# Recommender kernel on one core: gathered rows laid out by field, and both DRAM copies of a block in one transfer

## The chip, the cores and the metric

The kernel runs on one core of one Trainium2 chip. The metric is device time in microseconds (us) of one execution; smaller is better. Before the change three runs took 361.72, 362.16 and 364.56 us, median 362.16. One per cent of that is 3.6 us.

## The reference

512 samples have 32 fields each. Every field has its own table of rows of 16 numbers, and one row per sample and field is gathered. Then follow three interaction layers and a small multilayer perceptron, all in float32:

```python
e = jnp.stack([tbl_0[ids[:, 0]], tbl_1[ids[:, 1]], ...], axis=1)   # (512, 32, 16)
for W in (W0, W1, W2):                                             # W0 (32,32,64), W1 and W2 (32,64,64)
    xk = jax.nn.relu(jnp.einsum('bmd,bhd,mhk->bkd', x0, xk, W))
    outs.append(jnp.sum(xk, axis=2))                               # (512, 64) per layer
h = jnp.concatenate([z, dense_ctx], axis=1)                        # z is outs side by side, 192 wide
h = jnp.maximum(h @ W_top1 + b_top1, 0.0)                          # 512 wide
h = jnp.maximum(h @ W_top2 + b_top2, 0.0)                          # 256 wide
y = h @ W_top3
```

## The kernel before, in words

**Blocks.** The batch is cut into eight pairs of 32-sample chunks. Pairs 0 and 1 are worked in two halves each (blocks 0 to 3, 512 columns of sample times dimension, called half-width or narrow); pairs 2 to 7 are one block each (blocks 4 to 9, 1024 columns, wide). Each block goes through layers 0, 1 and 2; a step is written (layer, block), and the tuple `BEGUN` (L53) is the order of the 30 steps on VectorE and TensorE. Even pairs use one set of SBUF buffers, odd pairs the other ("streams").

**A step.** VectorE (DVE, `product`, L760) multiplies tiles of x0 with a factor that lies in PSUM and writes `vz`; GpSimd (POOL, L705) makes some of these products into `pz`; TensorE (PE, `contract`, L993) multiplies them with the weights and sums up in `acc`; ScalarE (ACT, L876) takes the relu, and L887 sends the result round to all partitions as `hidden`. Some factors are spread by TensorE instead (L924), for blocks 1 to 3 in layer 0 at L938, and for block 0 straight from the gathered rows (L960, L963). DVE sums over the 16 dimensions at L810. The numbers of tiles that each engine takes, and the gathers between them, are tables (`POOL_TILES`, `GATHERS_IN`, `PACED`, `BEHIND_SPREAD`) that the change leaves alone.

**Gathering.** POOL adds to every id the first row of its field's table (`index`, L709, one operation on all 128 columns) and issues 128 indirect transfers (L678). One brings a row of 16 floats to each of the 128 partitions: 32 fields times four quarters of a block's samples. A wide block has 16 of them, a narrow one 8. Partition `q * 32 + m` holds field m of quarter q.

**The DRAM scratch.** The operands of the products need each field's whole row on four or more partitions. So SyncE's queue (SP) writes every block's gathered rows to DRAM as 32 rows by field, twice (`scratch`, L558; the second copy stands behind the first, so that a read rotated by r fields does not wrap), and reads them back with access patterns that repeat or rotate fields:

```python
for c in range(1 if b in DIRECT else 2):
    copy = fields_dram[b][c * FIELDS:(c + 1) * FIELDS, :]
    sp.dma_start(copy.rearrange("m (q x) -> q m x", q=QUART), quarter_rows(b)) ...
```

`layer0_operands` issues `own` (L574, needs the first copy), `opposite` (L582, needs the second), and for wide blocks four `rotated` tiles (L593); `field_tiles` issues eight `fields_sb` tiles (L614). Rotated and field tiles are sent with at most three in flight: the fourth waits until the first has landed. All of this stands in one queue in the order of `LOADS` (L105): a wait in it holds back all that stands behind, and that order has `scratch 4, operands 4, fields 3, scratch 5, operands 5, fields 4`.

**Opposite fields.** Layer 0 uses symmetry; the pair of fields m and m + 16 is made by POOL (`opposite_product`, L688, into `oz`) from the gathered rows and `opposite`, and contracted with `w0c_sb` (L989), whose rows follow the partition layout of the gathered rows.

Of the kernel before, what the change touches and what calls it, by code (L numbers as in the profile page):

```python
# [11 lines left out]
P = 128  # L12
# [19 lines left out]
BLOCKS = [(pair, half * N, N, half * GATHERS // 2, GATHERS // 2) for pair in range(2) for half in range(2)]  # L32
BLOCKS += [(pair, 0, PAIR, 0, GATHERS) for pair in range(2, PAIRS)]
# [4 lines left out]
def stream(b):  # L38
    return BLOCKS[b][0] % STREAMS

# [339 lines left out]
def cin_dlrm(nc, table, ids, first_row, unit, turned, across, w0a, w0b, w0c, w1, w2, wt1, bt1, wt2,  # L380
             bt2, wt3, wt1_dense, dense, out):
    with ExitStack() as ctx:
# [6 lines left out]
        def sem(name):  # L389
            return ctx.enter_context(nc.semaphore(name))  # L390
# [6 lines left out]
        first_sb = sb("first_sb", [P, 1], I32)  # L397
# [15 lines left out]
        w0c_sb = sb("w0c_sb", [P, QUART, HID])  # L413
# [28 lines left out]
        scratch_in = [[sem(f"scratch_in{b}_{c}") for c in range(1 if b in DIRECT else 2)] for b in range(len(BLOCKS))]  # L442
# [64 lines left out]

        def landed(b):

            return 16 * (turn(b) + 1)  # L510
# [26 lines left out]
        def _(sp):  # L537
# [7 lines left out]
            sp.dma_start(w0c_sb[:, :, :], w0c).then_inc(w0_in, 16)  # L545
# [6 lines left out]
            def scratch(b):  # L552

                pair, _, _, first, rows = BLOCKS[b]
                sp.wait_ge(rows_in[b], 16 * rows)
                for c in range(1 if b in DIRECT else 2):
                    copy = fields_dram[b][c * FIELDS:(c + 1) * FIELDS, :]
                    sp.dma_start(copy.rearrange("m (q x) -> q m x", q=QUART),  # L558
                                 quarter_rows(b)) \
                      .then_inc(scratch_in[b][c], 16)  # L560

            def layer0_operands(b):
                _, col, cols, _, _ = BLOCKS[b]
                span, s = fields_dram[b], stream(b)
                sp.wait_ge(scratch_in[b][0], 16)
# [6 lines left out]
                if second_half(b):  # L572
# [23 lines left out]
            def field_tiles(b):  # L596
# [6 lines left out]
                sp.wait_ge(scratch_in[b][0], 16)  # L603
# [42 lines left out]
        def _(pool):  # L646
# [6 lines left out]
            def gather(i):  # L653
# [3 lines left out]
                if j == 0 and pair >= GRING:  # L657
                    before = max(a for a in range(len(BLOCKS)) if BLOCKS[a][0] == pair - GRING)
                    for a in range(before):
                        if BLOCKS[a][0] == pair - GRING:  # L660
                            pool.wait_ge(vz_ready, vectors_to((0, a)))
                            pool.wait_ge(scratch_in[a][0], 16)
                            if a not in DIRECT:
                                pool.wait_ge(pz_ready, pools_to((0, a)))
                                pool.wait_ge(scratch_in[a][1], 16)
                    pool.wait_ge(scratch_in[before][0], 16)
                    if before in DIRECT + BURST:
                        pool.wait_ge(vz_ready, vectors_to((0, before)))
                    if before not in DIRECT:
                        pool.wait_ge(scratch_in[before][1], 16)  # L670
                        pool.wait_ge(pz_ready, pools_to((0, before)))
# [4 lines left out]
                if i in BEHIND_SPREAD:  # L676
                    pool.wait_ge(factor_spread, BEHIND_SPREAD[i])
                nc.gpsimd.indirect_dma_start(  # L678
# [13 lines left out]
            def product(step, u):  # L692
# [10 lines left out]
                if at >= PRING:  # L703
# [210 lines left out]
        def _(pe):  # L914
# [52 lines left out]
            def contract(step, who, u, start, stop):  # L967
# [17 lines left out]
                if layer == 0 and t == L0TILES:  # L985
                    pieces = []
                    for q in (0, 2, 1, 3):
                        part = slice(q % 2 * quarter, (q % 2 + 1) * quarter)
                        last = nc.tensor.matmul(acc_of(step, q // 2)[:, part], w0c_sb[:, q, :], quarters,  # L989
# [167 lines left out]
```

## Time and profile before

| what | us |
|---|---|
| median of three runs | 362.16 |
| span of the profiled execution, first to last instruction | 340.6 |
| median less span (start and end of the program; the page gives no other time of the profiled execution) | 21.6 |
| TensorE busy | 304.3 (89%) |
| VectorE busy | 281.9 (83%) |
| GpSimd busy | 245.8 (72%) |
| ScalarE busy | 49.1 (14%) |
| SP's queue waiting for the DRAM copies before `own` (L574) | 26.6 |
| DVE at L760 waiting for `fields_sb` / for `rotated` | 5.2 / 1.8 |

Busy time is the sum of an engine's instructions. Idle time of an engine is put down to what released it. All instants below are counted from the span's start.

### The profile page before, as it was taken

How to read it: one execution, taken by the hardware profiler on the slowest of the kernel's cores; microseconds unless marked ns; L12 is line 12 of the kernel's file. 1: busy time of each engine (PE TensorE's matmuls, PEld its weight loads, DVE VectorE, ACT ScalarE, POOL GpSimd, SP SyncE). 2: the span in 40 equal slices, each digit the busy share in tenths (PEclk: the TensorE clock that was granted, in tenths of full speed). 3: DMA queues.
4: the chain of work that ended last, by engine and by line, in shares of the span. 5: the costliest groups of instructions: out<-in, count | busy, mean ns of one | idle time of the engine just before them, and what ended most of it. 6: DMA issues, size and time to landing. Idle time of an engine off the chain costs nothing.

```text
span 340.6 us, 4674 instructions
## 1 busy us (share of the span) xinstructions
PE 304.3 (89%) x1798; PEld 126.1 (37%) x1798; DVE 281.9 (83%) x172; ACT 49.1 (14%) x70; POOL 245.8 (72%) x194
## 2 busy tenths in 40 slices
PE   0198888989968898989999999999999999999997
PEld 0164554644423253233333333233333333333334
DVE  0038899999969799999999999989998879999210
ACT  1010002110111110110211301220131012020011
POOL 4656777877756878899979598979977678649200
PEclk9997999999989999999999999999999999999999
DMA  6264865738768888685899994943898996230000
GB/s 188 47 194 100 248 184 178 223 71 244 230 185 258 309 283 291 225 253 173 285 346 308 330 320 138 287 130 108 259 365 305 310 289 175 39 102 0 2 0 0
DMA packets 34040, 67.96 MB, mean 200 GB/s; under 512 B 5602, under 2 KB 14946, under 8 KB 34018
## 3 DMA queue, kind: packets, MB, share of 16 engines
q1 hardware_dynamic: 23298, 56.64, 49.9%
q10 hardware_dynamic: 6624, 9.96, 10.3%
q0 software_dynamic: 4096, 1.06, 3.7%
q8 instruction: 14, 0.23, 0.3%
q14 instruction: 8, 0.07, 0.1%
HBM read 55.38 MB, written 2.03 MB: 169 GB/s over the span
## 4 chain that ended last, share of the span: by engine, by line
PE 44%; DMA 25%; DVE 17%; issue 7%; POOL 2%; SPq 2%; ACTq 1%; ACT 1%; DVEq 1%
PE acc L993 34%; DVE vz L760 16%; DMA fields_sb<-fields 12%; DMA rotated<-fields 5%; DMA fields<-gathered 3%; DMA hidden<-relu_out 3%; POOL gathered L678 2%; PE factor L1005 2%; PE factor L924 2%; DMA gathered<-in_table,index 2%; PE factor L960 1%; PE factor L1000 1%; PE acc L989 1%; PE factor L938 1%; DVE feats L810 1%
## 5 line engine op out<-in xcount | busy, mean ns | idle before, releaser
L760 DVE TENSOR_TENSOR vz<-fields_sb,factor 128x1024 f32<-128x1024 f32 (+3 forms) x113 | 230.7, 2092 | 15.4 <-PE factor L924 8.0
L993 PE MATMUL acc<-vz,w_sb 128*64 128x512 f32 (+1 forms) x1232 | 227.5, 509 | 16.6 <-DVE vz L760 15.7
L678 POOL DMA_INDIRECT gathered<-in_table,index x128 | 121.6, 950 | 45.1 <-issue 27.8
L993 PEld LDWEIGHTS acc<-vz,w_sb 128*64 128x64 f32 x1232 | 87.5, 140 | 142.3 <-issue 90.0
L705 POOL TENSOR_TENSOR pz<-fields_sb,hidden 128x1024 f32<-128x1024 f32 (+1 forms) x52 | 118.0, 2291 | 23.3 <-DMA hidden<-relu_out 9.0
L993 PE MATMUL acc<-pz,w_sb 128*64 128x512 f32 (+1 forms) x208 | 50.7, 579 | 0.7 <-POOL pz L705 0.7
L876 ACT ACTIVATE relu_out<-acc 128x512 f32<-128x512 f32 (+1 forms) x30 | 15.3, 511 | 152.4 <-PE acc L993 123.7
L845 ACT ACTIVATE factor<-hidden 128x1024 f32<-128x1024 f32 (+1 forms) x23 | 20.1, 879 | 69.5 <-DVE vz L760 34.1
L760 DVE TENSOR_TENSOR vz<-rotated,factor 128x2048 f32<-128x2048 f32 x12 | 27.0, 2282 | 3.0 <-DMA rotated<-fields 1.8
L993 PEld LDWEIGHTS acc<-pz,w_sb 128*64 128x64 f32 x208 | 14.8, 137 | 29.9 <-issue 24.2
L810 DVE TENSOR_REDUCE feats<-relu_out 128x32 f32<-128x512 f32 (+1 forms) x30 | 17.2, 573 | 6.6 <-ACT relu_out L876 6.5
L960 PE MATMUL factor<-gathered,unit_sb 32*128 32x128 f32 x8 | 1.6, 493 | 15.4 <-DMA gathered<-in_table,index 15.4
L924 PE MATMUL factor<-relu_out,unit_sb 32*128 32x512 f32 (+1 forms) x68 | 11.0, 539 | 0.5 <-ACT relu_out L876 0.5
L777 DVE TENSOR_TENSOR vz<-own,factor 128x512 f32<-128x512 f32 x2 | 1.4, 689 | 11.2 <-ACT own L851 11.2
L989 PE MATMUL acc<-oz,w0c_sb 128*64 128x256 f32 (+1 forms) x72 | 8.2, 348 | 0.5 <-POOL oz L688 0.5
L845 ACT ACTIVATE factor<-own 128x1024 f32<-128x1024 f32 x6 | 6.2, 1026 | 13.4 <-POOL pz L705 8.5
L859 ACT ACTIVATE hidden<-factor 128x1024 f32<-128x1024 f32 (+1 forms) x4 | 3.7, 919 | 24.4 <-PE factor L924 24.4
L824 DVE TENSOR_SCALAR vz<-factor,bt_sb 128x512 f32<-128x512 f32 x2 | 1.5, 751 | 6.7 <-PE factor L1012 6.7
L960 PEld LDWEIGHTS factor<-gathered,unit_sb 32*128 32x128 f32 x8 | 1.0, 306 | 15.4 <-issue 15.4
L989 PEld LDWEIGHTS acc<-oz,w0c_sb 128*64 128x64 f32 x72 | 4.7, 137 | 5.4 <-issue 2.9
L924 PEld LDWEIGHTS factor<-relu_out,unit_sb 32*128 32x128 f32 x68 | 3.7, 183 | 7.7 <-issue 6.8
L729 DVE TENSOR_TENSOR w_sb<-vz 128x256 f32<-128x256 f32 x1 | 0.4, 425 | 7.0 <-DMA w0c_sb<-in_w0c 7.0
(36 smaller groups left out, 61.9 us busy)
## 6 DMA issues: line engine op xcount, KB each, us to landing
fields_sb<-fields SPq DMA_DIRECT2D x48, 512.0 KB, 5.7
rotated<-fields SPq DMA_DIRECT2D x24, 512.0 KB, 6.0
fields_sb<-fields SPq DMA_DIRECT2D x32, 256.0 KB, 3.5
hidden<-relu_out ACTq DMA_DIRECT2D x30, 256.0 KB, 5.4
own<-fields SPq DMA_DIRECT2D x6, 512.0 KB
gathered<-in_table,index POOLq DMA_INDIRECT x128, 4.1
hidden<-relu_out ACTq DMA_DIRECT2D x16, 128.0 KB, 4.3
fields<-gathered SPq DMA_DIRECT2D x12, 128.0 KB
```

Of the source, the lines that this page charges most:

```text
L678: nc.gpsimd.indirect_dma_start(gathered[:, pair % GRING, j, :], None, table, bass.IndirectOffsetOnAxis(ap=index[:, i:i + 1], axis=0)).then ...
L705: nc.gpsimd.tensor_tensor(pz[:, at % PRING, 0:cols], fields[s][:, t, col:col + cols], hidden_of(step, g), ALU.mult).then_inc(pz_ready, 1)
L760: nc.vector.tensor_tensor(vz[:, at:at + nt, 0:cols].rearrange("p t (a n) -> p t a n", n=half), src[:, t:t + nt, col:col + cols].rearrange( ...
L810: nc.vector.tensor_reduce(feats[layer][:, pair, first:first + count], relu_of(step).rearrange("p (b d) -> p b d", d=DIM), op=ALU.add, axis ...
L845: nc.scalar.activation(factor_of(step, g), src.rearrange("p (a n) -> p a n", a=2), ACT.Copy).then_inc(factor_put, 1)
L859: nc.scalar.activation(hidden_of(step, g).rearrange("p (a n) -> p a n", a=2), factor_of(step, g), ACT.Copy).then_inc(hidden_copied, 1)
L876: nc.scalar.activation(relu_of(step), acc[:, n % 2, 0:half], ACT.Relu).then_inc(relu_done, 1)
L924: last = nc.tensor.matmul(factor_of(step, g)[:, ab, :], unit_sb[row:row + HROWS, :], relu_of(before)[row:row + HROWS, :], start=True, stop ...
L960: last = nc.tensor.matmul(slot_of(step, held)[:, ab, wave * quarter:(wave + 1) * quarter], by, rows[row, :], start=True, stop=True)
L989: last = nc.tensor.matmul(acc_of(step, q // 2)[:, part], w0c_sb[:, q, :], quarters, start=False, stop=q % 2 == 1)
L993: last = nc.tensor.matmul(acc_of(step, ab), w_sb[layer][:, kt, :], z[:, ab * half:(ab + 1) * half], start=start and j == 0, stop=stop and ...
L1005: return nc.tensor.matmul(to, wt2_sb[:, k, m * P:(m + 1) * P], rows, start=k == 0, stop=k == F_TOP1 // P - 1)
```

## The change

Wide blocks (`by_field(b)` is 1) now have field m, quarter q on partition `4 * m + q`. The ids are sorted that way on the host, `first_row` has a second column for this layout, and `w0c_sb` holds a second version. For these blocks partition p's part lies at DRAM offset p * 256 elements, so one transfer with 128 partitions as its outer dimension writes both copies (256 runs of 1 KB), and `opposite` is read with the same outer 128. Narrow blocks keep their layout; their copies are written in four transfers of 32 partitions, each for both copies (one copy for block 0). There is one semaphore per block, so `own` now waits for both copies. The index addition is split: 32 columns first, the other 96 after the first 21 gathers.

```diff
-                for c in range(1 if b in DIRECT else 2):
-                    copy = fields_dram[b][c * FIELDS:(c + 1) * FIELDS, :]
-                    sp.dma_start(copy.rearrange("m (q x) -> q m x", q=QUART),
-                                 quarter_rows(b)) \
-                      .then_inc(scratch_in[b][c], 16)
+                cols, span, n = BLOCKS[b][2], fields_dram[b], scratch_copies(b)
+                if by_field(b):
+                    twice = bass.AP(span.tensor, span.offset,
+                                    [[cols // QUART, P], [FIELDS * cols, n], [1, cols // QUART]])
+                    sp.dma_start(twice, quarter_rows(b)[:, None, :].broadcast_to([P, n, cols // QUART])) \
+                      .then_inc(scratch_in[b], 16)
+                    return
+                for q in range(QUART):
+                    twice = bass.AP(span.tensor, span.offset + q * (cols // QUART),
+                                    [[cols, FIELDS], [FIELDS * cols, n], [1, cols // QUART]])
+                    mine = quarter_rows(b)[q * FIELDS:(q + 1) * FIELDS, None, :]
+                    sp.dma_start(twice, mine.broadcast_to([FIELDS, n, cols // QUART])).then_inc(scratch_in[b], 16)
...
-                sp.wait_ge(scratch_in[b][0], 16)
+                sp.wait_ge(scratch_in[b], copied(b))
...
-                sp.wait_ge(scratch_in[b][1], 16)
                 far = bass.AP(span.tensor, span.offset + FIELDS // 2 * cols,
-                              [[quarter, QUART], [cols, FIELDS], [1, quarter]])
+                              [[quarter, P], [1, quarter]] if by_field(b)
+                              else [[quarter, QUART], [cols, FIELDS], [1, quarter]])
...
-            nc.gpsimd.tensor_tensor(index[:, :], ids_sb[:, :], first_sb[:, :].broadcast_to([P, PAIRS * GATHERS]),
-                                    ALU.add).then_inc(index_ready, 1)
+            narrow = NARROW_PAIRS * GATHERS
+            nc.gpsimd.tensor_tensor(index[:, 0:narrow], ids_sb[:, 0:narrow],
+                                    first_sb[:, 0:1].broadcast_to([P, narrow]), ALU.add).then_inc(index_ready, 1)
             pool.wait_ge(index_ready, 1)
             for i in range(FIRST_GATHERS):
                 gather(i)
+            nc.gpsimd.tensor_tensor(index[:, narrow:], ids_sb[:, narrow:],
+                                    first_sb[:, 1:2].broadcast_to([P, PAIRS * GATHERS - narrow]),
+                                    ALU.add).then_inc(index_ready, 1)
...
+        def copied(b):
+            return 16 if by_field(b) else 16 * QUART
```

How instructions move. SP's queue, from the first copy of block 0 to block 1's reads, before (L558 is the copy; `4x32x128` is its DRAM side):

```order
L558 DMA fields<-gathered 4x32x128 [waits rows_in0]
L614 DMA fields_sb<-fields 128x1x512 [waits scratch_in0_0]
...
L558 DMA fields<-gathered 4x32x128 [waits rows_in1]
L558 DMA fields<-gathered 4x32x128
L574 DMA own<-fields 128x1x512 [waits scratch_in1_0]
L582 DMA opposite<-fields 128x1x128 [waits scratch_in1_1]
```

and the same place with the change (L580 is the copy of a narrow block, L594 `own`, L602 `opposite`):

```order
L580 DMA fields<-gathered 32x128 [waits rows_in0]
L580 DMA fields<-gathered 32x128 x3
L634 DMA fields_sb<-fields 128x1x512 [waits scratch_in0]
...
L580 DMA fields<-gathered 32x2x128 [waits rows_in1]
L580 DMA fields<-gathered 32x2x128 x3
L594 DMA own<-fields 128x1x512 [waits scratch_in1]
L602 DMA opposite<-fields 128x1x128
```

Block 0 issues four copies instead of one, blocks 1 to 3 four instead of two, and `opposite` has no wait of its own any more. At the first wide block (block 4) SP's queue has with the change (L573 is the copy, L613 `rotated`):

```order
L573 DMA fields<-gathered 128x2x256
L594 DMA own<-fields 128x1x1024
L602 DMA opposite<-fields 128x256
L613 DMA rotated<-fields 128x1x1024 x4
L634 DMA fields_sb<-fields 128x1x512 x8
```

where two copies of form `4x32x256` stood. GpSimd, from the index addition to block 1's opposite product, with the change:

```order
L730 TENSOR_TENSOR index<-ids_sb,first_sb 128x32
L698 DMA gathered<-in_table,index 128x16 x21
L735 TENSOR_TENSOR index<-ids_sb,first_sb 128x96
L698 DMA gathered<-in_table,index 128x16 x2
L708 TENSOR_TENSOR oz<-gathered,opposite 128x128
L698 DMA gathered<-in_table,index 128x16 x11
```

Before, one addition of form 128x128 stood ahead of 23 gathers. TensorE, VectorE and ScalarE keep their instructions and their order.

## Rows read from the trace of the kernel before

**Rows 1.** Busy time by stretch: us, PE, PEld, DVE, ACT, POOL, PE clock, DMA share, GB/s

```profile
90.00:105.00 15.00, 11.42 (x80) 5.46 (x80) 11.46 (x11) 1.30 (x2) 9.70 (x11) 0.89 0.65 189
105.00:120.00 15.00, 12.28 (x78) 4.81 (x76) 13.15 (x10) 2.39 (x4) 12.07 (x14) 1.00 0.85 292
120.00:140.00 20.00, 19.07 (x128) 8.55 (x124) 20.00 (x12) 3.04 (x4) 15.15 (x14) 1.00 0.87 296
180.00:200.00 20.00, 20.00 (x98) 6.82 (x96) 20.00 (x10) 4.20 (x5) 16.56 (x9) 1.00 0.97 312
260.00:280.00 20.00, 19.15 (x98) 6.36 (x96) 16.04 (x8) 2.22 (x3) 14.14 (x7) 1.00 0.91 304
```

**Rows 2.** VectorE in order of time: start, us, instruction, [idle before, releaser]

```profile
50.40 2.35 DVE L800 TENSOR_TENSOR vz<-own,factor 128x1024 f32<-128x1024 f32 x2 [0.63 <-DMA own<-fields]
...
95.21 1.22 DVE L760 TENSOR_TENSOR vz<-fields_sb,factor 128x1024 f32<-128x1024 f32 x1 [1.18 <-DMA fields_sb<-fields]
98.09 1.22 DVE L760 TENSOR_TENSOR vz<-fields_sb,factor 128x1024 f32<-128x1024 f32 x1 [1.66 <-DMA fields_sb<-fields]
99.59 2.88 DVE L760 TENSOR_TENSOR vz<-fields_sb,factor 128x1024 f32<-128x1024 f32 x2 [0.28 <-DMA fields_sb<-fields]
...
114.87 2.29 DVE L760 TENSOR_TENSOR vz<-rotated,factor 128x2048 f32<-128x2048 f32 x1 [1.84 <-DMA rotated<-fields]
```

**Rows 3.** SP's queue in order of time: start, us of issuing, transfer, count

```profile
15.30 0.69 SPq L558 DMA_DIRECT2D fields<-gathered  x1
17.84 7.86 SPq L614 DMA_DIRECT2D fields_sb<-fields  x8
29.33 1.17 SPq L558 DMA_DIRECT2D fields<-gathered  x2
32.00 0.56 SPq L574 DMA_DIRECT2D own<-fields  x1
32.81 0.54 SPq L582 DMA_DIRECT2D opposite<-fields  x1
...
42.06 1.17 SPq L558 DMA_DIRECT2D fields<-gathered  x2
47.56 0.56 SPq L574 DMA_DIRECT2D own<-fields  x1
...
72.67 1.17 SPq L558 DMA_DIRECT2D fields<-gathered  x2
76.16 0.56 SPq L574 DMA_DIRECT2D own<-fields  x1
77.51 0.54 SPq L582 DMA_DIRECT2D opposite<-fields  x1
78.10 7.35 SPq L593 DMA_DIRECT2D rotated<-fields  x4
85.54 10.98 SPq L614 DMA_DIRECT2D fields_sb<-fields  x8
96.57 1.17 SPq L558 DMA_DIRECT2D fields<-gathered  x2
```

**Rows 4.** Chain of waits between 76 and 116 us: start, us, what

```profile
78.10 6.82 DMA rotated<-fields
...
108.35 6.40 DMA rotated<-fields
```

**Rows 5.** Busy time by stretch, columns as in rows 1: two copies' transfers

```profile
72.70:76.00 3.30, 3.01 (x26) 1.66 (x26) 3.30 (x5) 0.38 (x1) 2.48 (x3) 1.00 0.22 52
206.30:209.60 3.30, 3.30 (x18) 1.11 (x16) 3.30 (x2) 0.00 (x0) 2.67 (x4) 1.00 0.25 53
```

**Rows 6.** GpSimd in order of time

```profile
3.35 0.40 POOL L709 TENSOR_TENSOR index<-ids_sb,first_sb 128x128 int32<-128x128 int32 x1 [2.90 <-DMA first_sb<-in_first_row]
...
37.00 0.47 POOL L688 TENSOR_TENSOR oz<-gathered,opposite 128x128 f32<-128x128 f32 x1
...
93.28 0.74 POOL L688 TENSOR_TENSOR oz<-gathered,opposite 128x256 f32<-128x256 f32 x1
```

More of the change, by code:

```diff
@@ L28 @@
 TOP_LOADS = 9 * 16
-BLOCKS = [(pair, half * N, N, half * GATHERS // 2, GATHERS // 2) for pair in range(2) for half in range(2)]
-BLOCKS += [(pair, 0, PAIR, 0, GATHERS) for pair in range(2, PAIRS)]
+NARROW_PAIRS = 2
+BLOCKS = [(pair, half * N, N, half * GATHERS // 2, GATHERS // 2) for pair in range(NARROW_PAIRS) for half in range(2)]
+BLOCKS += [(pair, 0, PAIR, 0, GATHERS) for pair in range(NARROW_PAIRS, PAIRS)]
 LAST = len(BLOCKS) - 1
@@ L39, in stream, with by_field, scratch_copies @@
     return BLOCKS[b][0] % STREAMS
+def by_field(b):
+    return int(BLOCKS[b][0] >= NARROW_PAIRS)
+def scratch_copies(b):
+    return 1 if b in DIRECT else 2
 def blocks_before(b):
@@ L412, in cin_dlrm @@
         across_sb = sb("across_sb", [P, P])
-        w0c_sb = sb("w0c_sb", [P, QUART, HID])
+        w0c_sb = sb("w0c_sb", [P, 2, QUART, HID])
         w_sb = [sb("w0_sb", [P, L0TILES, HID]),
@@ L441, in cin_dlrm @@
         rows_in = [sem(f"rows_in{b}") for b in range(len(BLOCKS))]
-        scratch_in = [[sem(f"scratch_in{b}_{c}") for c in range(1 if b in DIRECT else 2)] for b in range(len(BLOCKS))]
+        scratch_in = [sem(f"scratch_in{b}") for b in range(len(BLOCKS))]
         own_in = [sem(f"own_in{s}") for s in range(STREAMS)]
@@ L544, in _ @@
             sp.dma_start(w0b_sb, w0b).then_inc(w0_in, 16)
-            sp.dma_start(w0c_sb[:, :, :], w0c).then_inc(w0_in, 16)
+            sp.dma_start(w0c_sb[:, :, :, :], w0c).then_inc(w0_in, 16)
             sp.dma_start(w_sb[1][:, :, :], w1).then_inc(w1_in, 16)
@@ L661, in gather @@
                             pool.wait_ge(vz_ready, vectors_to((0, a)))
-                            pool.wait_ge(scratch_in[a][0], 16)
+                            pool.wait_ge(scratch_in[a], copied(a))
                             if a not in DIRECT:
                                 pool.wait_ge(pz_ready, pools_to((0, a)))
-                                pool.wait_ge(scratch_in[a][1], 16)
-                    pool.wait_ge(scratch_in[before][0], 16)
+                    pool.wait_ge(scratch_in[before], copied(before))
                     if before in DIRECT + BURST:
@@ L677, in gather @@
                     pool.wait_ge(factor_spread, BEHIND_SPREAD[i])
+                if i == NARROW_PAIRS * GATHERS:
+                    pool.wait_ge(index_ready, 2)
                 nc.gpsimd.indirect_dma_start(
@@ L988, in contract @@
                         part = slice(q % 2 * quarter, (q % 2 + 1) * quarter)
-                        last = nc.tensor.matmul(acc_of(step, q // 2)[:, part], w0c_sb[:, q, :], quarters,
+                        last = nc.tensor.matmul(acc_of(step, q // 2)[:, part], w0c_sb[:, by_field(b), q, :], quarters,
                                                 start=False, stop=q % 2 == 1)
@@ L1095 @@
                      .reshape(ids[pair].shape))
-    ids = np.ascontiguousarray(ids.transpose(1, 3, 0, 2).reshape(P, PAIRS * GATHERS))
-    first_row = np.ascontiguousarray(np.tile(first.astype(np.int32), QUART)[:, None])
+    ids = np.concatenate([ids[:NARROW_PAIRS].transpose(1, 3, 0, 2).reshape(P, NARROW_PAIRS * GATHERS),
+                          ids[NARROW_PAIRS:].transpose(3, 1, 0, 2).reshape(P, (PAIRS - NARROW_PAIRS) * GATHERS)],
+                         axis=1)
+    first_row = np.stack([np.tile(first.astype(np.int32), QUART), np.repeat(first.astype(np.int32), QUART)], axis=1)
     w0 = np.asarray(inputs["L0_rec_W0"])
```

12 lines of the change are left out of this document (6 added, 6 removed).

## The prediction, made before the changed kernel ran

> **What bounds the kernel now.** I read the busy time by stretch first, because an average over the whole span (TensorE 89%, VectorE 83%) hides that the bound moves. From 120 us on some engine is always full: VectorE has 20.00 of 20 us in 120 to 140, both engines have 20.00 in 180 to 200, and in 260 to 280 VectorE is down to 16.04 while TensorE has 19.15 [rows 1]. Moving transfers there can give back at most TensorE's missing 0.85. Between 90 and 120 neither is full: VectorE 11.46 and 13.15 of 15, TensorE 11.42 and 12.28, and TensorE's granted clock falls to 0.89 in 90 to 105 [rows 1]. So I asked VectorE's order of time what it waits for there: three waits for field tiles of block 3 (1.18 + 1.66 + 0.28 = 3.12 us) and one for a rotated tile of block 5 (1.84 us); earlier there is one of 0.63 for block 2's `own` [rows 2]. These 5.59 us are what faster transfers can win; everything behind them is an unbroken row of full engines, so a microsecond won there should reach the end.
>
> Why are the tiles late? SP's queue has them behind the copies and operands of block 4. The copies are issued at 72.67, `own` at 76.16, `opposite` at 77.51, the four rotated tiles from 78.10, and only at 85.54 the field tiles of block 3 [rows 3]. In the chain of waits the first rotated tile alone takes 6.82 us to land, and the last rotated tile of block 5, issued at 108.35, takes 6.40, which is what VectorE waits for at 114.87 [rows 4, 2].
>
> **What the copies cost.** While only the copies of a wide block are on their way, the 16 DMA engines are busy 22% and 25% of the time and move 52 and 53 GB/s [rows 5]; the full machine moves 312 [rows 1]. A share of a quarter is what four of sixteen engines give, and the copy's DRAM side has 4 as its outer dimension; the field tiles, whose sides have 32 and 128 outermost, fill the engines to 0.97 [rows 1]. So I take four engines for the old copies and the old `opposite` (4 outermost), and sixteen for the new ones (128 or 32). The Trainium skill (DMA: Bandwidth & Descriptors, "Why a DMA increments its semaphore by 16 and not by 1") says that a transfer is spread over the largest number up to 16 that divides the outermost sizes of both its sides. By that rule the numbers are the same four and sixteen; the trace agrees in the quarter share, but shows no copy in the new form.
>
> Two rows give the size. Block 0's copy (64 KB, so 16 KB for each of four engines) holds the queue from 15.30 to 17.84, 2.54 us. Block 4's first copy (128 KB, 32 KB each) holds it from 72.67 to 76.16, 3.49 us [rows 3]. The difference, 0.95 us, is the price of 16 KB per engine; the rest, 1.59, is issue and latency.
>
> **Wide blocks.** One transfer now carries 256 KB; over sixteen engines that is 16 KB each, the same as block 0's. `own` then goes out 2.54 us after the copy instead of 3.49: 0.95 earlier. `opposite` follows at once, 0.65 behind (issue 0.54 to 0.56 and a gap), at 3.19 instead of 77.51 - 72.67 = 4.84: 1.65 earlier, and so are the rotated tiles. Bounds of this: no gain at all if the engines do not spread; 1.35 us later for `own` if the two copies go one behind the other as now (77.51 - 76.16); and 2.6 earlier if the data took nothing. The measured pair of rows is nearest.
> `opposite` itself loads the four engines with 32 KB instead of 8; those 24 KB are 24/16 x 0.95 = 1.4 us by which the first rotated tile behind it lands late. How much of the 6.82 us is that, the trace doesn't say, because `own` and other transfers stand in the same queues. Bounds 0 and 1.4; I take 0.7, the middle, since nothing favours an end. So the rotated tiles of block 4, and block 3's field tiles behind them, start 1.65 + 0.7 = 2.35 earlier.
> POOL takes 0.25 of this back: block 4's rows are gathered by a POOL that issues without a pause, and the second index addition stands before them. The two `oz` rows give 0.47 us for 128 columns and 0.74 for 256, or 0.0021 per column [rows 6]; 96 columns of the index cost 0.40 - 32 x 0.0021 = 0.33 us, of which about 0.1 is covered because the engine waits less before the next gather after an arithmetic operation. Net: 2.1 us earlier.
> VectorE's 3.12 us of waits shrink by these **2.1 us**. The rotated tile of block 5 gains the 2.1 us, then once more the 2.35 of its own block: 4.4, while VectorE comes 2.1 earlier. The difference of 2.3 is more than the 1.84 of that wait: **1.84 us**. If VectorE does not pause, TensorE does not either, and its low clock in 90 to 105 may go; I count nothing for it, since VectorE's wait for it is 0.41 or less, to be bounded at that.
>
> **Start.** The first index addition has 32 columns: 96 x 0.0021 = **0.2 us** less on the path to the first gather.
>
> **Narrow blocks.** Four issues of about 0.6 us (two took 1.17) instead of one or two. The last of four starts 1.8 us after the first, its 32 KB are 2 KB per engine (0.12 us), and 1.59 is fixed: 3.5 us in all. Block 0: 3.5 against 2.54, 0.95 later, for field tiles that VectorE uses from 26.2 us on, eight us after the first goes out; the last two tiles have least slack. Bounds 0 and 0.95. Block 1: `own` 3.5 instead of 32.00 - 29.33 = 2.67 after, 0.8 later, needed at about 36 when it would land; bounds 0 and 0.8. Block 2: `own` comes 5.5 us after the copies now (42.06 to 47.56), because three field tiles stand ahead in the queues; the four issues end before that, so the queues decide, and either the wait of 0.63 goes or it grows by 0.8. Block 3's `own` isn't waited for. Together I take **0.3 us** of loss, nearer to nothing than to the sum of 2.55, because no row before shows VectorE waiting for block 0 or 1.
> The rows of field tiles, eight issued in 7.86 us with a landing behind each [rows 3], show transfers on this queue that overlap, so the four copies are priced as overlapping.
>
> **Late.** `own`, `opposite` and rotated tiles of blocks 8 and 9 are also earlier, and field tiles behind them. TensorE lacks 0.85 us in 260 to 280 [rows 1]: bounds 0 and 0.85, I take **0.3 us**. `w0c_sb` is 128 KB larger, but TensorE begins with gathered rows long after the weights. The rest of the transfers on SP are the same.
>
> **Sum.** -2.1 - 1.84 - 0.2 + 0.3 - 0.3 = -4.1 us. The profiled execution's span of 340.6 becomes 336.5. The 21.6 us between span and median are left as they are: 362.16 - 4.1 = 358.1; I say **358.0**. What a measurement of this kernel can tell from no change is about 1%, 3.6 us, so below 358.5 is faster.
>
> **Rivals.**
> 1. *The transfers were the whole problem.* All 5.59 us of waits go, TensorE's low clock with them (0.41), 0.85 late and 0.2 at the start: 7.0 us, 355.1. For it: the hot four engines also delay `own`. Against: block 3's tiles would have to start 3.1 us earlier. Chance 0.10.
> 2. *Hidden, or given back.* The field tiles are late because 512 KB tiles fill the queues (DMA share 0.85 in 105 to 120), not because of the copies, and the fixed pacing tables were made for other arrival times; only 1 or so is left: 361.5. For it: the queue's share is high from 105 on. Against: 0.65 in 90 to 105, and a quarter during the copies. Chance 0.22.
> 3. *The copies do not spread.* One transfer of 256 KB moves at the old 53 GB/s (the write to DRAM, not the number of engines, sets it). `own` then waits for both copies, 4.84 - 0.6 = 4.24 us instead of 3.49, and the narrow blocks' extra issues show in full: +0.75 and +2.55 less 0.2, so +3.1 us, 365.3. It decides as soon as `own` of block 4 goes out more than 3.49 us after its copy. Against: the quarter share is too neat. Chance 0.08. A rule of the Trainium skill speaks for a loss here too (SBUF — State Buffer, "The DMA setup-cost knee" and "Can I just issue two DMAs to hit both halves?"): each transfer pays a roughly fixed 2 us, and splitting by partitions wins nothing. Taken without overlap, an estimate by that page is 6 us more per narrow block; the trace's overlapping field tiles speak against it.
> The forecast itself has 0.60; with half of its uncertain terms either way it spans 355.9 to 360.3, and somewhat over half of that is below 358.5.
>
> **Numbers.** Range 354.9 to 362.6: the forecast's span, rival 1 and rival 2 to no change; outside are rival 3 and what I haven't thought of. Faster: 0.36 of the forecast and all of rival 1, with a little of rival 2, 0.49. Slower by over 1%: part of rival 3, 0.06. Same: 0.45.
>
> **What would show it.** In the changed kernel: (a) `own` of block 4 about 2.5 us behind its copy, `opposite` 0.65 behind `own`; DMA share well over 0.25 in that gap. (b) block 3's field tiles start about 10.5 us after block 4's copy instead of 12.87. (c) VectorE's waits for field tiles before 100 us fall from 3.12 to about 1, and the one for `rotated` is gone. (d) Block 0's first field tile 3.5 us after its copy, and no new wait of VectorE over 0.5 us before 60. (e) the clock share of the 90 to 105 stretch rises towards 1.00. What would make it wrong: (a) true but the waits of (c) replaced by waits for ScalarE's relays or POOL's products of the same length.

## The result and the profile after the change

| | us |
|---|---|
| changed kernel, median of 20 runs (range) | 362.00 (358.86 to 365.74) |
| kernel before, same chip, median of 20 runs (range) | 364.44 (361.41 to 369.03) |
| ratio, 95% interval | 0.9944 (0.9918 to 0.9971) |
| profiled execution of the changed kernel: its time, its span | 360.27, 358.4 |

The ratio is that of the runs within about 1.5% of each kernel's fastest; the medians are of all. The change gives 0.56% or 2.0 us (0.3 to 0.8%), half of the 4.1 that were forecast. One number of this table has nothing to do with the change: time less span is 1.9 us here, and it was 21.6 for the profile on which the forecast was built. The profile after, in the order of rows 1 to 6. Busy time by stretch (us, PE, PEld, DVE, ACT, POOL, PE clock, DMA share, GB/s), answering to rows 1:

```profile
90.00:105.00 15.00, 12.42 (x90) 6.76 (x92) 11.87 (x11) 1.34 (x4) 8.38 (x9) 0.89 0.83 272
105.00:120.00 15.00, 11.24 (x82) 6.22 (x84) 11.87 (x10) 1.82 (x3) 9.65 (x12) 0.89 0.66 188
120.00:140.00 20.00, 15.48 (x104) 6.43 (x102) 18.07 (x14) 2.99 (x5) 13.77 (x15) 1.00 0.77 260
180.00:200.00 20.00, 20.00 (x100) 6.86 (x98) 18.99 (x9) 4.28 (x5) 17.49 (x15) 1.00 0.84 278
260.00:280.00 20.00, 20.00 (x96) 6.70 (x94) 18.47 (x9) 4.90 (x6) 18.51 (x10) 1.00 0.97 337
```

From 90 to 140 us no engine is full. Before, VectorE was from 120 on [rows 1]. The granted clock of 90 to 105 is 0.89 as it was, and 105 to 120 has it too. VectorE in order of time, the long waits up to 125 us (rows 2):

```profile
40.22 2.48 DVE L819 TENSOR_TENSOR vz<-own,factor 128x512 f32<-128x512 f32 x4 [4.54 <-remote]
...
58.52 2.35 DVE L824 TENSOR_TENSOR vz<-own,factor 128x1024 f32<-128x1024 f32 x2 [4.37 <-issue]
...
74.97 2.35 DVE L824 TENSOR_TENSOR vz<-own,factor 128x1024 f32<-128x1024 f32 x2 [3.99 <-remote]
...
97.15 1.75 DVE L784 TENSOR_TENSOR vz<-fields_sb,factor 128x1536 f32<-128x1536 f32 x1 [2.47 <-PE acc L1017]
...
122.21 6.67 DVE L784 TENSOR_TENSOR vz<-rotated,factor 128x2048 f32<-128x2048 f32 x3
```

No wait for a field or rotated tile is left up to 125 us, but three of 4 to 4.5 us stand in front of VectorE's first products of blocks 1, 2 and 3, where rows 2 had 0.63 at most. The 3.00 us before 111.54, put down to an unknown source ("remote"), end on the semaphore that TensorE's `contract` moves. For the three waits the view names no instruction either. In the trace VectorE waits there for the result of a burst of short TensorE matmuls (L962, more under e9): the last matmul record of block 1's burst ends at 34.81, the semaphore that announces the burst's result moves only at 40.14, and VectorE goes on at 40.22. SyncE's queue, the part that rows 3 showed:

```profile
14.89 1.73 SPq L580 DMA_DIRECT2D fields<-gathered  x4
17.89 7.49 SPq L634 DMA_DIRECT2D fields_sb<-fields  x8
28.63 2.76 SPq L580 DMA_DIRECT2D fields<-gathered  x4
32.58 0.52 SPq L594 DMA_DIRECT2D own<-fields  x1
...
84.68 0.39 SPq L573 DMA_DIRECT2D fields<-gathered  x1
86.88 0.53 SPq L594 DMA_DIRECT2D own<-fields  x1
87.46 0.59 SPq L602 DMA_DIRECT2D opposite<-fields  x1
88.09 5.62 SPq L613 DMA_DIRECT2D rotated<-fields  x4
93.83 12.32 SPq L634 DMA_DIRECT2D fields_sb<-fields  x8
```

`own` of block 4 follows its copy by 2.20 us, `opposite` `own` by 0.58, block 3's field tiles the copy by 9.15. But the copy itself goes out at 84.68, not at 72.67 [rows 3]. While it is on its way the DMA share is 0.49 at 148 GB/s, against 0.22 and 52 [rows 5]; other transfers run beside it:

```profile
84.70:86.90 2.20, 2.05 (x20) 0.95 (x16) 2.20 (x4) 0.00 (x0) 1.59 (x3) 1.00 0.49 148
```

GpSimd's first addition, its first gather and its second addition, answering to rows 6:

```profile
3.02 0.24 POOL L730 TENSOR_TENSOR index<-ids_sb,first_sb 128x32 int32<-128x32 int32 x1 [2.57 <-DMA first_sb<-in_first_row]
3.54 1.11 POOL L698 DMA_INDIRECT gathered<-in_table,index  x1 [0.28 <-POOL index L730]
...
34.58 0.36 POOL L735 TENSOR_TENSOR index<-ids_sb,first_sb 128x96 int32<-128x96 int32 x1
```

### The profile page after: what moved, and what is told of

The parts are those of the page before. It is cut to its first block, busy times and chain, and to the rows that moved or that the text cites. A ratio compares the mean times of both kernels' runs of the same rounds, so it can differ in the third digit from the quotient of the medians.

```text
span 358.4 us, 4675 instructions
## 1 busy us (share of the span) xinstructions
PE 310.9 (87%) x1798; PEld 128.9 (36%) x1798; DVE 282.1 (79%) x172; ACT 49.3 (14%) x70; POOL 246.0 (69%) x195
## 4 chain that ended last, share of the span: by engine, by line
PE 64%; issue 11%; POOL 10%; DVE 8%; another core or an unknown queue 3%; DMA 1%; ACT 0%; DVEq 0%; SPq 0%; POOLq 0%
PE acc L1017 56%; DVE vz L784 7%; POOL gathered L698 6%; POOL pz L725 4%; PE factor L948 2%; PE factor L1029 2%; PE factor L1024 1%; PE acc L1013 1%; PE factor L984 1%; PE factor L1036 1%; DVE vz L824 1%; DMA gathered<-in_table,index 1%; DVE vz L819 1%; DMA first_sb<-in_first_row 0%
## 5 line engine op out<-in xcount | busy, mean ns | idle before, releaser
L1017 PE MATMUL acc<-vz,w_sb 128*64 128x512 f32 (+1 forms) x1232 | 232.9, 516 | 22.2 <-DVE vz L784 9.2
L1017 PEld LDWEIGHTS acc<-vz,w_sb 128*64 128x64 f32 x1232 | 90.4, 143 | 150.1 <-issue 114.5
L824 DVE TENSOR_TENSOR vz<-own,factor 128x1024 f32<-128x1024 f32 x4 | 4.7, 1218 | 8.4 <-issue 4.4
L708 POOL TENSOR_TENSOR oz<-gathered,opposite 128x256 f32<-128x256 f32 (+1 forms) x9 | 5.8, 645 | 1.4 <-remote 1.3
```

What stands on the lines that cost most here:

```text
L708: nc.gpsimd.tensor_tensor(oz[:, 0:quarter], quarter_rows(step[1]), opposite[s][:, at:at + quarter], ALU.mult).then_inc(pz_ready, 1)
L824: nc.vector.tensor_tensor(made.rearrange("p t (q x) -> p t q x", q=QUART), whole.rearrange("p (q x) -> p q x", q=QUART)[:, None, :, :] .br ...
L1017: last = nc.tensor.matmul(acc_of(step, ab), w_sb[layer][:, kt, :], z[:, ab * half:(ab + 1) * half], start=start and j == 0, stop=stop and ...
```

## The experiments

### Two ends of the program, read in every run

VectorE has the same 172 instructions in the same order in all kernels here. Three of them are marks, given here by their start in the repeated kernel before: A (232.50), the first field-tile product behind the reduction at 231.90; C (278.23), its first product of layer 1 of block 8; and B (346.04), the first operation of the perceptron. By the order of steps A falls in layer 1 of block 7. So start to A holds the narrow blocks and most of blocks 4 to 7, A to B the rest of these and all of blocks 8 and 9, and C to B layers 1 and 2 of blocks 8 and 9. "New" and "old" are the form of copies and `opposite`.

| kernel | blocks 4-7 | blocks 8, 9 | start to A | A to B | C to B |
|---|---|---|---|---|---|
| before, first profile | old | old | 214.41 | 113.33 | 67.47 |
| e0_before | old | old | 232.50 | 113.54 | 67.81 |
| e2_narrow_only | old | old | 233.90 | 113.32 | 67.95 |
| e6_early | new | old | 234.02 | 113.29 | 67.43 |
| e10_before_four | old | old | 228.90 | 113.19 | 65.86 |
| after | new | new | 234.75 | 110.81 | 65.86 |
| e3_after | new | new | 230.95 | 111.00 | 65.86 |
| e1_wide_only | new | new | 233.90 | 111.81 | 65.86 |
| e5_late | old | new | 233.17 | 111.51 | 65.86 |
| e9_four_matmuls | new | new | 229.24 | 111.45 | 65.86 |
| e7_far124 | new, `opposite` in two | same | 235.73 | 110.51 | 66.19 |
| e8_one_in_flight | new | new | 259.24 | 111.75 | 65.86 |
| e4_copy124 | new, copy in two (124 + 4) | same | 229.03 | 116.24 | 70.22 |

Ratios below have their 95% interval and are against the kernel before on the same chip. The diffs are shortened.

### e0_before: the kernel before once more

No edit.

> The kernel before, unchanged, against itself: ratio 1.000 for every theory; it sets how far two equal kernels can be told apart. Its profile tells two theories of the missing gain apart. Theory A (the first profile of before is not a typical execution: its span of 340.6 us stands 21.6 under the median, while the changed kernel's span of 358.4 stands only 1.9 under its own time): the span here is about 360 us, with TensorE crawling after the burst spreads of blocks 1 to 3, as in the changed kernel's profile (idle of VectorE of 4 us each at 40, 58 and 75 us). Theory B (the change itself brings those stalls, and the wide blocks' gain pays for them): the span here is about 341 us and they are absent.

Measured: ratio 1.0065 (1.0033 to 1.0096), span 358.9. A kernel against itself comes out 0.65% off, so an interval here doesn't cover all that moves a total. And the repeat's profile doesn't look like the first: of 81 later executions of the kernel before none has a span under 356.7 us. Busy time by stretch, first profile:

```profile
36.00:40.00 4.00, 4.00 (x38) 2.33 (x36) 2.52 (x5) 0.38 (x1) 3.33 (x4) 1.00 0.74 202
55.00:60.00 5.00, 4.09 (x36) 2.32 (x36) 5.00 (x6) 0.00 (x0) 3.78 (x5) 1.00 0.83 263
```

and the repeat:

```profile
36.00:40.00 4.00, 2.40 (x9) 0.66 (x10) 0.83 (x1) 0.00 (x0) 2.48 (x4) 1.00 0.72 215
55.00:60.00 5.00, 2.77 (x16) 1.24 (x15) 1.17 (x2) 0.28 (x2) 4.63 (x5) 1.00 0.31 85
```

In the repeat TensorE issues 9 matmuls instead of 38 in the same four microseconds, at full clock. VectorE waits for the burst in front of them: from the burst's start to VectorE's first product from it there are 5.55, 5.78 and 4.17 us for blocks 1, 2 and 3, where the first profile has 1.95, 2.25 and 1.29. GpSimd, whose gathers are paced by this work, comes later too, and block 4's copy goes out at 83.08 instead of 72.67. The repeat's VectorE:

```profile
40.35 2.48 DVE L795 TENSOR_TENSOR vz<-own,factor 128x512 f32<-128x512 f32 x4 [3.53 <-issue]
...
58.83 2.35 DVE L800 TENSOR_TENSOR vz<-own,factor 128x1024 f32<-128x1024 f32 x2 [4.17 <-issue]
...
94.77 1.75 DVE L760 TENSOR_TENSOR vz<-fields_sb,factor 128x1536 f32<-128x1536 f32 x1 [1.69 <-PE acc L993]
...
121.30 6.67 DVE L760 TENSOR_TENSOR vz<-rotated,factor 128x2048 f32<-128x2048 f32 x3
...
283.48 3.35 DVE L760 TENSOR_TENSOR vz<-fields_sb,factor 128x3072 f32<-128x3072 f32 x1 [1.30 <-DMA fields_sb<-fields]
...
297.90 3.35 DVE L760 TENSOR_TENSOR vz<-fields_sb,factor 128x3072 f32<-128x3072 f32 x1 [1.08 <-DMA fields_sb<-fields]
```

The field and rotated waits of 85 to 125 us are absent **without** the change: VectorE comes so late that the tiles are there. Two waits for field tiles stand at 283 and 298, 2.38 us together; the first profile has them too, 1.18 at 265.39 and 0.88 at 279.61.

### e1_wide_only and e2_narrow_only: the two halves of the change

e1 has the wide blocks' part of the diff (one copy transfer, `opposite` over 128, field-major partitions, the split addition) and writes narrow blocks as before. e2 has only the narrow part:

```diff
-  for c in range(copies): sp.dma_start(copy c, 128 partitions)
+  for q in range(QUART): sp.dma_start(both copies of quarter q, 32 partitions)     # e2; wide blocks as before
```

> Only the wide blocks are changed (rows by field and quarter, both copies in one transfer, opposite read with 128 outermost, index addition split); blocks 0 to 3 keep one or two copies with 4 outermost and one wait per copy. If the wide blocks bring the gain and the narrow ones cost a little (forecast: -4.4 and +0.3 us), this is 0.2 to 0.5 us faster than the changed kernel: ratio to before about 0.993. If the narrow blocks' sixteen engines are where the gain is, ratio 1.000.

> Only the narrow blocks are changed (four transfers of 32 partitions, each for both copies); wide blocks, their layout and the index addition stay as before. By my forecast +0.3 us, ratio 1.001, with block 0's field tiles starting about 0.95 us later behind its copy. If the narrow blocks carry the gain: ratio 0.995.

Measured: e1 0.9921 (0.9876 to 0.9965), A to B 111.81; e2 0.9971 (0.9937 to 1.0006), A to B 113.32, with the late waits still there (1.23 at 284.45, 1.30 at 299.07). The gain of the late part belongs to the wide blocks. In e2 block 0's field tiles follow the copy by 2.92 us (2.54 in e0_before), block 1's `own` by 4.25 (2.50). No cost of that delay can be seen: start to A, 233.90 and 232.50, differs by less than two runs of the changed kernel do (234.75 and 230.95).

### e3_after: the changed kernel once more

No edit of the changed kernel.

> The changed kernel again, beside the parts: ratio 0.994 as first measured, to be compared with the parts on the same chip. A second profile tells which stalls of its first profile repeat.

Measured: 0.9828 (0.9768 to 0.9889, of six runs only), span 354.8, beside 0.9944 in the first measurement. The two intervals of one and the same kernel don't meet. In the profiles the 3.8 us between them lie before A; A to B repeats to 0.2. Part of this may be TensorE's granted clock: in 60 to 65 us it is 0.50 in the first profile of the changed kernel, 0.80 in this one and 1.00 in e4's. So what separates forms has to be read by parts. Busy time from A to B, e0_before (its DVE waits for fields are above):

```profile
232.50:346.04 113.54, 110.66 (x519) 37.65 (x516) 96.76 (x46) 17.45 (x22) 79.52 (x41) 1.00 0.55 173
```

and e3_after:

```profile
230.95:341.95 111.00, 110.35 (x521) 37.16 (x518) 96.49 (x46) 17.67 (x22) 79.85 (x41) 1.00 0.56 172
```

Same work on every engine, 2.54 us less time. TensorE lacked 2.88 us in the first and 0.65 in the second. It is idle for 0.98 of the 2.88 where VectorE waited for the field tile (and for 0.53 behind VectorE's second such stretch; the remaining 1.34 are a wait for GpSimd's opposite product):

```profile
286.89 2.79 PE L993 MATMUL acc<-vz,w_sb 128*64 128x512 f32 x12 [0.98 <-DVE vz L760]
```

C to B repeats to 0.01 us where no late wait for fields falls into it. The stretch in e0_before, in e3_after, and in two experiments below, e10 and e4:

```profile
278.23:346.04 67.81, 66.30 (x311) 22.88 (x308) 53.24 (x26) 8.73 (x12) 41.55 (x18) 1.00 0.43 132
276.09:341.95 65.86, 65.86 (x311) 22.16 (x308) 53.06 (x26) 8.77 (x12) 40.00 (x17) 1.00 0.42 123
276.23:342.09 65.86, 65.86 (x311) 22.15 (x308) 53.05 (x25) 8.73 (x12) 39.50 (x17) 1.00 0.42 123
275.05:345.27 70.22, 67.77 (x311) 22.47 (x308) 53.14 (x26) 8.75 (x12) 43.54 (x19) 0.98 0.47 134
```

All six profiles in which blocks 8 and 9 have the new form uncut take 65.86 us, with TensorE full in the one shown. The four with the old form and two late waits for fields (2.02 to 2.53 us together) take 67.43 to 67.95, 1.8 more on average. A late wait of 0.68 (e7) goes with 66.19, one of 2.77 (e4) with 70.22. And e10 has the old form but no late wait for fields, and takes 65.86 like the new one: there VectorE reaches C 29.8 us after block 9's copy went out, against 28.0 in e0_before and e3_after, and the tiles are in time. So it is these waits, and not the form as such, that cost the time behind C.

### e5_late and e6_early: new form for blocks 8 and 9 alone, and for 4 to 7 alone

```diff
-            return int(BLOCKS[b][0] >= NARROW_PAIRS)
+            return int(6 <= BLOCKS[b][0] < 8)      # e5_late; e6_early: 2 <= ... < 6
```

Other wide blocks keep the two copies and `opposite` of before; narrow blocks as changed.

> The changed kernel with the new layout, the single transfer and the new opposite only for blocks 8 and 9; blocks 4 to 7 have the form of before. Theory L (the gain is made late: VectorE's two waits for field tiles of block 8 and 9, 1.30 and 1.08 us in the second profile of before, go): the whole gain is here, about -2.4 us, ratio 0.993, and those two waits are gone. My prediction's theory E (the gain is made at blocks 4 and 5, -3.9 us): ratio 0.999.

> The mirror: new form for blocks 4 to 7 only, blocks 8 and 9 as before. Theory L: ratio 1.000, and VectorE's waits for field tiles after 280 us stay at about 2.4 us together, though block 3's field tiles start 9.2 us after block 4's copy and not 11.7. Theory E: ratio 0.989.

Measured: e5 0.9922 (0.989 to 0.9954), A to B 111.51, no late wait for fields. e6 0.9893 (0.9838 to 0.9948), A to B 113.29, late waits 1.10 at 284.93 and 0.92 at 299.18. By parts the two are clear: blocks 8 and 9 carry what A to B gains, and the new form in blocks 4 to 7 gives nothing there. Whether it gives something before A isn't: e6's total is low, but its start to A of 234.02 is not (e5: 233.17).

### e4_copy124: the wide copies made to use few engines

```diff
-                    sp.dma_start(twice, quarter_rows(b) ... [P, n, ...])
+                    for lo, hi in ((0, 124), (124, P)):
+                        sp.dma_start(twice[lo:hi], quarter_rows(b)[lo:hi] ... [hi - lo, n, ...])
```

> The changed kernel, but each wide copy is cut into a transfer of 124 partitions and one of 4, so that its outer size is divisible by 4 and not by 16. Layout, bytes and the single wait stay. If the number of engines follows the outer size, the 256 KB go over four engines again: own goes out about 5.3 us after the copy (1.6 + 62/16 x 0.95), against 2.2 to 2.4 in the changed kernel and 3.5 before; DMA share about 0.25 meanwhile. If merging into one transfer or the linear DRAM order made it faster, it is 2.8 (one more issue). In time: ratio about 1.000 by the first, 0.993 by the second.

Measured: 0.9965 (0.9927 to 1.0004). SyncE's queue at block 4:

```profile
81.17 0.79 SPq L577 DMA_DIRECT2D fields<-gathered  x2
86.91 0.53 SPq L598 DMA_DIRECT2D own<-fields  x1
87.48 0.60 SPq L606 DMA_DIRECT2D opposite<-fields  x1
88.14 6.80 SPq L617 DMA_DIRECT2D rotated<-fields  x4
95.46 10.87 SPq L638 DMA_DIRECT2D fields_sb<-fields  x8
```

and the stretch in which the copy is on its way:

```profile
81.20:86.90 5.70, 4.70 (x38) 2.26 (x34) 5.70 (x6) 0.19 (x1) 3.78 (x4) 1.00 0.30 69
```

`own` waits 5.74 us instead of 2.20 for the same 256 KB, at a DMA share of 0.30 and 69 GB/s instead of 0.49 and 148. The second issue explains 0.4 us of it (0.79 against 0.39). 3.5 us more for 48 KB more per engine (64 on each of four against 16 on each of sixteen, if the copies use four and sixteen) is the forecast's price of 0.95 us per 16 KB, within a quarter. The Trainium skill's rule by the divisor of the outermost size, which the forecast cited, gives four engines for 124 (DMA: Bandwidth & Descriptors, "Why a DMA increments its semaphore by 16 and not by 1"), and the 5.74 agrees. VectorE's late wait for fields is 2.77 at 281.77, and A to B is 116.24: 5.0 above the new form's mean. Late, a slower copy costs time; early, start to A is 229.03 although block 3's field tiles go out 14.29 us behind block 4's copy, and that is the shortest start to A of all kernels that keep the burst, the first profile apart. It is a single profile, but it shows that a slower early copy needn't delay anything.

### e7_far124: `opposite` cut 124 + 4

```diff
-                sp.dma_start(opposite[s][:, at:at + quarter], far)
+                for lo, hi in ((0, 124), (124, P)):
+                    sp.dma_start(opposite[s][lo:hi, at:at + quarter], far[lo:hi])
```

> The changed kernel, but opposite of the wide blocks is read in 124 + 4 partitions, four engines again; copies stay as changed. By my forecast opposite's four engines cost the rotated tiles 0.7 us (bounds 0 and 1.4) plus 0.6 for the second issue: block 3's field tiles start 9.8 to 11.2 us after block 4's copy (9.2 changed, 11.7 before). Time: ratio 0.994 to 1.000.

Measured: 0.9876 (0.9824 to 0.9928). Block 3's field tiles go out 10.03 us behind block 4's copy, against 9.15 and 9.19 in the changed kernel's two profiles. 0.32 of the 0.86 is the second issue (`opposite` takes 0.89 instead of 0.59, and its successor starts 0.94 behind it instead of 0.63), so about 0.5 is what an `opposite` on few engines costs the transfers behind it; the forecast took 0.7 between 0 and 1.4. A late wait of 0.68 for fields is back at 298.11, but A to B is 110.51.

### e9_four_matmuls and e10_before_four: TensorE's burst shortened

Layer 0 of blocks 1 to 3 begins with a burst: 16 calls of `matmul` with 128 columns, which the trace records as 32 matmuls and 32 loads of weights, 64 instructions in 1.17 us. VectorE's long waits are for the result of these. Here four matmuls of 512 columns take the place of each sixteen; the values of blocks 1 to 3 are then not the reference's.

```diff
-                for t in range(L0TILES):
-                    for q in range(QUART):
-                        matmul(bank(q)[:, t * quarter:(t + 1) * quarter], turned_sb[row, t, :], rows[row, :])
+                for q in range(QUART):
+                    matmul(bank(q), turned_sb[row, 0, :], rows[row, None, :].broadcast_to([FIELDS, L0TILES, quarter]))
```

> The changed kernel, but the layer 0 spread of blocks 1 to 3 is made by 4 matmuls of 512 columns instead of 16 of 128, on the same 32-row groups: the same columns, a quarter of the instructions. (All four tiles then hold the first rotation, so the values of those blocks are not the reference's.) Theory I (TensorE's instructions run dry behind a burst of 64 short ones: 9 matmul records in 36 to 40 us where the first profile of before has 38): the slow stretches of about 4 us behind each of the three bursts go, the span falls by 8 to 12 us, ratio about 0.97. Theory M (it is the transfers' load or the memory, not the burst): nothing changes, ratio 0.99, slow stretches stay.

> The kernel before with the same 4 matmuls per spread (values of blocks 1 to 3 as above). By theory I it comes near the first profile of before (span 340.6 instead of 359): ratio about 0.975. Against e9 it gives the worth of the change in a kernel that runs as the profile I predicted from: 4.1 us if my sum was right for that profile, 2.4 to 3 if only the late blocks gain.

Measured: e9 (the changed kernel so edited) 0.9843 (0.9794 to 0.9892), span 353.6; e10 (the kernel before so edited) 0.9864 (0.9806 to 0.9922), span 354.9. Busy time by stretch in e9:

```profile
36.00:40.00 4.00, 4.00 (x38) 2.45 (x36) 3.68 (x6) 0.00 (x0) 3.27 (x4) 1.00 0.90 273
55.00:60.00 5.00, 3.95 (x38) 2.18 (x34) 4.81 (x5) 1.80 (x4) 4.54 (x5) 1.00 0.46 122
```

TensorE has as many matmuls in these stretches as in the first profile (38 and 38, there 38 and 36), with transfers loading the engines as much as before or more (0.90). From the burst's start to VectorE's first product from it there are 1.95, 3.13 and 1.95 us in e9 and 2.57, 4.30 and 1.64 in e10, against 4.2 to 6.7 in the nine profiles that keep the burst (after, e0 to e7) and 1.95, 2.25 and 1.29 in the first. So the number of instructions in the burst has a part in the delay. It isn't the whole cause: the first profile has the same 64 instructions and not the delay, and block 2's stays in part without them. Nor is a load of instructions seen: the trace's two instruction queues move nothing between 31.5 and 48 us in e0_before.

What the delays cost is less clear. Start to A is 229.24 and 228.90, some 4 us less than the 233.3 that seven ordinary profiles (after, e0 to e3, e5, e6) average, but e4 has 229.03 with all three delays (6.33, 5.72 and 4.35). e10's total is 1.4% below the kernel before, clear of the interval; e9's ratio, 0.9843, isn't below e3's. Old and new copies give the same start to A here, so no early gain of the wide copies shows, and the two medians, 358.44 and 359.51, are 1.1 us apart with intervals that overlap. The first profile had 214.41. Some 15 of its 19 us aren't found again by shortening the burst, and stay unexplained.

A to B has to be read with care in e10: its 113.19 are not made by late waits for fields. It loses 1.6 us before C, behind a wait of TensorE for GpSimd's opposite product (1.44 us at 245.94), where the granted clock is 0.60 in 246 to 250.

### e8_one_in_flight: fewer transfers at a time

```diff
-                flying = IN_FLIGHT_DIRECT if b in DIRECT else IN_FLIGHT
+                flying = 1 if b in HALVES else IN_FLIGHT
```

> The changed kernel, but the field tiles of the half-width blocks go one at a time (the next is issued when the one before has landed) instead of up to three in flight; values unchanged. Two theories on the slow stretches of TensorE behind the three burst spreads (12, 10 and about 15 TensorE instructions in 36 to 40, 55 to 60 and 70 to 75 us of the changed kernel's profile, against 38, 36 and 31 in the first profile of before). Theory D: transfers in flight slow TensorE's supply of instructions (they share the DMA engines or the memory). Then these stretches hold 25 or more instructions each, and VectorE's waits of about 4 us at 40, 58 and 75 us fall below 2. Theory B: they come from the burst of 64 short instructions itself. Then the stretches stay at 9 to 18 instructions and the waits at 3 to 4.5 us; blocks 1 to 3 then run up to 1 or 2 us later by their later tiles, and the time is between 360 and 364 us.

Measured: 1.0519 (1.0451 to 1.0588), 384.2 us. Neither theory had that size. VectorE now waits for field tiles themselves, 4.65 us at 35.43 and 4.75 at 41.39, and for `own`:

```profile
73.07 2.35 DVE L824 TENSOR_TENSOR vz<-own,factor 128x1024 f32<-128x1024 f32 x2 [8.22 <-DMA own<-fields]
```

so it can't be told from these stretches what slowed TensorE. TensorE's order of time is a little help: behind the first burst it ran on at full rate (20 matmuls in 2.38 us from 48.35) and VectorE's product followed the burst's start by 3.75 us, behind the second it had gaps again (4 in 0.66 from 66.18, 3 in 0.65 from 67.65). Theory D isn't decided by it; what the run does show is that one in flight is too few in the narrow blocks (two weren't tried). A to B, 111.75, is untouched by 25 us of delay before it.

## Why the direction was right and the size was not

**Direction and range came out, the size did not.** Forecast -4.1 us, measured -2.0; 362.00 is 0.6 inside the range's upper end. That the direction came out is luck in the main: the terms that carried 3.94 of the 4.1 gave nothing that can be seen, and a term taken at 0.3 gave the gain. Step by step:

- **The sum's base: failed.** "The 21.6 us between span and median are left as they are." That was the step. In every later execution the gap is 1.8 to 2.2, so those 21.6 us were 18 us of execution that the first profile didn't have: it was not a faster copy of the ordinary run, but one with other waits. The argument that a row of full engines carries every early microsecond to the end fails with it: in 120 to 140 us, where VectorE had 20.00 of 20, it has 18.07 in the changed kernel's profile, and TensorE 15.48. The two largest terms, 2.1 for block 3's field tiles and 1.84 for the rotated tile, stand on waits that the repeated kernel before doesn't have. Together they are 3.94 of the 4.1, and nothing of them is seen: the four profiles with new form in blocks 4 to 7 (after, e3, e1, e6) average 233.4 from start to A, the three with the old form (e0, e2, e5) 233.2, with a spread of 3.8 among equals. A gain under 1 us there can't be excluded.
- **Four engines against sixteen: right.** `own` 2.20 and 2.37 behind the copy (forecast 2.54; the kernel before 3.49 and 3.50), `opposite` 0.58 behind `own` (0.65), block 3's field tiles 9.15 and 9.19 (10.5; before 12.87 and 11.70). e4 speaks for the number of engines as the cause: one transfer's bytes and layout, cut at 124, are slow again. No view here counts the engines of one transfer; the number is inferred from the DMA shares and these times.
- **The late term: right in kind, a seventh of its size.** 0.3 was taken, at most 0.85, because "TensorE lacks 0.85 us in 260 to 280" [rows 1]. Measured from A to B: 113.33 is the mean of five profiles with the old form in blocks 8 and 9, 111.26 that of seven with the new one, e4 left out: 2.1 us, with spreads of 0.35 and 1.3. This is as much as the whole measured gain, and, e10 left out too, 1.8 of it lie between C and B, where the late waits for fields are. The bound was wrong because it took one stretch of 20 us for the 113 in which blocks 8 and 9 run: in the first profile TensorE lacks 2.39 us from A to B, and VectorE's waits for fields are 1.18 and 0.88 there. Both lie inside the stretch that was read, but the sum took only TensorE's idle time of that stretch and not the waits. This row of the first profile gives the idle time of the whole part:

```profile
214.41:327.74 113.33, 110.94 (x521) 37.76 (x518) 96.75 (x45) 17.60 (x22) 81.02 (x42) 1.00 0.56 176
```

- **Narrow blocks: size of the delay mixed, effect right.** Block 0's tiles came 3.00 us behind the copy (forecast 3.5), block 1's `own` 3.95 (forecast 3.5; the four issues took 2.76 us, not 1.8), block 2's 4.80 against 4.63. No wait of VectorE for a transfer of blocks 0 to 3 appeared. Four copies of 32 partitions issued in 1.73 us and landed within 3.00 of the first: they overlap, and the 6 us per narrow block that the forecast estimated from the Trainium skill (SBUF — State Buffer, "The DMA setup-cost knee") aren't there. That estimate was also too high for blocks 1 to 3, which have two transfers more and not three: 4 us by the same working.
- **Index: right.** 0.24 us instead of 0.40, and the first gather at 3.54 instead of 4.02, 0.33 of it because the ids came earlier (3.02 against 3.35 in [rows 6]); e0_before's VectorE starts its ninth instruction at 30.07, the changed kernel at 29.18 and 29.22.
- **Clock: counted at nothing, rightly.** It didn't rise in 90 to 105.
- **The rivals.** Rival 2 (361.5, hidden or given back) has a change of -0.7, not much nearer to -2.0 than the forecast. Its first reason, field tiles late for other causes, was not the one: early, the tiles are not late at all. Rival 3 fell with `own` at 2.20, rival 1 (7.0 us) with the measured 2.0.

What stays open: why the first profile ran without the delays, what holds back the result of a burst of short instructions, and whether the early blocks gain some tenths. Totals can't settle the last: equal kernels came out 0.65% and 1.2% apart.

The fastest version measured is the changed kernel itself (357.12 in e3_after; e9, which is not the same computation, had 358.44 with a shorter span). A burst with fewer, longer matmuls that computes the right values wasn't built; e10's ratio gives an estimate of some 5 us for it in the kernel before, e9 against e3 gives nothing in the changed one.

## What to carry to other kernels

Before costing anything, hold the profiled execution's span against the median: with a gap of 21.6 us, where every later execution has 1.8 to 2.2, the waits in that profile are those of another execution, and a second profile is worth more than any sum. Bound a gain by the idle time of the bounding engine over the whole part that the change touches, not over one slice, and ask for the waits in it. A DRAM copy of 128 KB with an outermost size of 4 held up its reader for 3.5 us, at a DMA share of 0.22 to 0.25; 256 KB with 128 on both sides took 2.2 to 2.4.

## What the runs showed of the hardware

- The result of a burst of 64 TensorE instructions, recorded in 1.17 us, reached VectorE 4.2 to 6.7 us after the burst's start in nine profiles, 1.6 to 4.3 us with four matmuls of 512 columns for each sixteen of 128, and 1.3 to 2.3 us in the one odd profile. In 36 to 40 us, behind the first burst, TensorE issued 9, 12 and 16 matmuls (e0_before, after, e3_after), against 38 and 31 in e9 and e10, at a granted clock of 1.00 and with nothing that it waits for in the trace ("issue").
- 256 KB in two transfers of 124 + 4 partitions took 5.74 us, in one of 128 partitions 2.20.
- One transfer of both copies issues in 0.38 to 0.40 us; two transfers took 1.17.
- The same program, unchanged, came out 1.0065 against itself, and the changed one 0.9828 and 0.9944.
